# Selective scans on one core: the rows of B and C start 8 bytes further on, and one weight a tile goes to the projections' PSUM bank

## The reference

```
# L1
dts, B, C = split(einsum('bkdl,kcd->bkcl', xs, x_proj_weight))       # 6, 16, 16 rows
delta = softplus(einsum('bkrl,kdr->bkdl', dts, dt_projs_weight) + bias)
h[l] = h[l-1] * exp(delta[l] * A) + (delta[l] * xs[l]) * B[l]         # per d and n
y[l] = sum over n of h[l] * C[l]
# L3
phi = exp(-cumsum(delta * A_log));  dbx = delta * B * xs
h = phi * cumsum(dbx / (phi + 1e-12));  y = einsum('bkdln,bknl->bkdl', h, C)
```

## Time and profile before

| | us |
|---|---|
| three executions | 16074.49, 16085.93, 16095.41; median 16085.93 |
| the profiled execution | 16072.64 |
| its span, from the first to the last instruction | 16070.6 |
| scans of L1, two pairs | 2333 to 5827 and 6058 to 9552 |
| scans of L3, two pairs | 10421 to 12850 and 13363 to 15780 |

### The profile page before, as it was taken

How to read it: one execution, slowest core, us unless ns; L and a number is a source line. 1 busy time by engine, 2 the same in 40 slices (tenths; PEclk the granted TensorE clock), 3 DMA queues, 4 the chain that set the end, 5 groups by cost and what they waited for, 6 DMA issues and landing times. The chain is left out here.

```text
span 16070.6 us, 187344 instructions
## 1 busy us (share of the span) xinstructions
PE 13492.7 (84%) x38048; PEld 5643.9 (35%) x38048; DVE 14447.3 (90%) x19631; ACT 12255.5 (76%) x27077; POOL 11724.6 (73%) x6313
## 2 busy tenths in 40 slices
PE   7998979999999978999999987877777777777777
PEld 2222224444444433444444434433333333333333
DVE  6666649999999989999999985799999989999998
ACT  3555568888888857888888864599999958989996
POOL 0000039999999979999999982388888857888886
PEclk9999989999999989999999997989889888888988
DMA  1100014444444434444444432123333212333221
GB/s 24 21 14 17 5 52 122 121 122 121 120 119 121 120 97 117 121 122 121 121 119 121 120 109 63 54 85 86 85 86 84 86 42 84 87 85 86 84 85 46
DMA packets 543192, 1404.82 MB, mean 87 GB/s; under 512 B 135566, under 2 KB 191926, under 8 KB 539430
## 3 DMA queue, kind: packets, MB, share of 16 engines
q1 hardware_dynamic: 542034, 1392.84, 30.9%
HBM read 1311.24 MB, written 58.30 MB: 85 GB/s over the span
## 5 line engine op out<-in xcount | busy, mean ns | idle before, releaser
L1085 PE MATMUL PS<-Hc,ident 128*128 128x448 f32 x16128 | 7145.1, 579 | 1391.7 <-POOL Hc L1434 1308.2
L1425 POOL TENSOR_TENSOR Tr<-du,BC 128x1344 f32<-128x1344 f32 x2688 | 6894.1, 2565 | 38.0 <-DVE du L1293 36.9
L1085 PEld LDWEIGHTS PS<-Hc,ident 128*128 128x128 f32 x16128 | 3044.4, 199 | 5375.3 <-issue 2719.2
L1434 POOL TENSOR_TENSOR Hc<-Hr,BC 128x896 f32<-128x896 f32 (+1 forms) x2688 | 4049.6, 1507 | 755.0 <-DVE Hr L1343 730.2
L1206 ACT ACTIVATE PS<-dl,A 128x448 f32<-128x448 f32 x5376 | 3399.0, 632 | 976.7 <-DVE Hr L1343 691.2
L1343 DVE TENSOR_TENSOR_SCAN Hr<-PS,Tr 128x449 f32<-128x449 f32 x2688 | 2879.7, 1071 | 1.6 <-ACT PS L1206 0.6
L1343 DVE TENSOR_TENSOR_SCAN PS<-PS,Tr 128x449 f32<-128x449 f32 x2688 | 2830.2, 1074 | 56.3 <-ACT PS L1206 48.5
L1350 DVE TENSOR_TENSOR Hc<-PS,BC 128x448 f32<-128x448 f32 x3584 | 2080.6, 600 | 0.0
L1216 ACT ACTIVATE PS<-cs,lneps,A 128x448 f32<-128x448 f32 x2688 | 1935.7, 720 | 78.3 <-DVE PS L1343 59.0
L1343 DVE TENSOR_TENSOR_SCAN Hr<-Ar,PS 128x449 f32<-128x449 f32 x1792 | 1930.5, 1077 | 0.0
L1325 DVE SCALAR_TENSOR_TENSOR PS<-PS,Tr 128x448 f32<-128x448 f32 x2688 | 1649.3, 614 | 132.6 <-ACT PS L1216 124.4
(11 more groups left out here) (271 smaller groups left out, 15421.6 us busy)
## 6 DMA issues: line engine op xcount, KB each, us to landing
BC<-bcscratch SPq DMA_DIRECT2D x5376, 224.0 KB, 3.6
zscratch<-zst SPq DMA_DIRECT2D x84, 224.0 KB, 1.9
bcscratch<-rows SPq DMA_DIRECT2D x336, 56.0 KB, 1.7
z<-zscratch SPq DMA_DIRECT2D x28, 672.0 KB, 4.9
xg<-mid SPq DMA_DIRECT2D x12, 1176.0 KB, 8.1
xr<-mid SPq DMA_DIRECT2D x56, 168.0 KB, 2.7
rl<-rows SPq DMA_DIRECT2D x56, 168.0 KB, 3.4
Q<-part SPq DMA_DIRECT2D x72, 98.0 KB, 4.3
```

Source lines behind the costliest of these rows:

```text
L1085: e.matmul(PS[:, YB + c, 0:T], K["ident"][:], Hc[:, g % NHC, c, :], start=False, stop=(nn == 15)).then_inc(y_done, 1)
L1425: e.tensor_tensor(Tr[:, g % NTR] if ratio else Tr[:, g % NTR, :, 1:TW], du[:, q % 2], b, ALU.mult).then_inc(t_done, 1)
L1434: e.tensor_tensor(Hc[:, g % NHC, m:3], Hr[:, g % NH, m - 1:2, 1:TW], c_, ALU.mult).then_inc(hp_done, 1)
```

## The change

Three parts, in `scans`:

1. `BC` gets rows of 452 elements, of which elements 2 to 449 are used: each row of B and of C begins 8 bytes behind a multiple of 16. A B row and its C row no longer adjoin in SBUF.
2. What PE writes to the bank XB begins at column 1 instead of 0 (`X`, the projection's rows, and their readers), in both layers.
3. In L3, the weight with s = 30 goes to the bank XB (`SPARE`), and the others share the ring of three. At s = 29 and s = 30 ACT is one unit further ahead with weights and decays, so that two of each are made before the Ln instead of one; `weight_before` gives the weight whose bank a weight takes. `total` of column 0 waits until the scan with s = 30 is done, since it writes over that weight. One memset more zeroes the column 0 of XB.

```diff
-        return PS[:, (XB, HB, 2 if ratio else HB + 1)[c] if q == 0 else XB, 0:T]
+        return PS[:, (XB, HB, 2 if ratio else HB + 1)[c] if q == 0 else XB, 1:1 + T]
...
-        BC = sb("BC", [128, NBS, 2, T])
+        BC = sb("BC", [128, NBS, 2, TP])[:, :, :, 2:2 + T]
...
+        def weight_bank(u):
+            q, r = divmod(u, 48)
+            return XB if r == SPARE else (u - q - (r > SPARE)) % NW
+
+        def weight_before(u):
+            n, back = 0, u
+            while n < NW:
+                back -= 1
+                n += back % 48 != SPARE
+            return back
...
             def total(q, c):
...
+                if ratio and q and c == 0:
+                    e.wait_ge(s_done, 48 * (q - 1) + SPARE + 1)
...
             def weight(u):
...
-                if u >= NW:
-                    e.wait_ge(s_done, u - NW + 1)
+                if u % 48 == SPARE:
+                    e.wait_ge(x_free, use(q + 1, "delta", 2) + 1 if q + 1 < NQS else use(q, "total", 2) + 1)
+                elif u >= NW:
+                    e.wait_ge(s_done, weight_before(u) + 1)
...
-                if ratio and u + 2 < NU:
-                    weight(u + 2)
-                while made < min(u + 3, NU):
+                ahead = u + 4 if ratio and s in (BURST, BURST + 1) and q + 1 < NQS else u + 3
+                while ratio and weighed < min(ahead, NU):
+                    weight(weighed)
+                    weighed += 1
+                while made < min(ahead, NU):
                     decay(made)
                     made += 1
```

More of the change, by code:

```diff
@@ L955, in scans @@
     TW, TP = T + 1, T + 4
+    BURST = 29
+    SPARE = BURST + 1
     NQS = NK * NT
@@ L1015, in input_at @@
         def input_at(g, c):
-            return PS[:, (3 * g + c) % NW, 0:TW] if ratio else Tr[:, g % NTR, c, :]
+            return PS[:, weight_bank(3 * g + c), 0:TW] if ratio else Tr[:, g % NTR, c, :]
         def state_at(g, c, first):
@@ L1035, in proj @@
                 for c in range(3):
-                    a = e.matmul(PS[0:76, XB, 0:T], xp[:, k % 2, c, :], xs[:, c, :], start=(c == 0), stop=(c == 2))
+                    a = e.matmul(PS[0:76, XB, 1:TW], xp[:, k % 2, c, :], xs[:, c, :], start=(c == 0), stop=(c == 2))
                 a.then_inc(x_full, 1)
@@ L1125, in keep_rows @@
                     e.wait_ge(rows_out, 32 * q)
-                e.activation(rows[:], PS[0:64, XB, 0:T], ACT.Copy).then_inc(x_free, 1)
+                e.activation(rows[:], PS[0:64, XB, 1:TW], ACT.Copy).then_inc(x_free, 1)
             def keep_dts(q):
@@ L1131, in keep_dts @@
                 e.wait_ge(x_full, use(q, "proj") + 1)
-                e.activation(dts[:], PS[64:76, XB, 0:T], ACT.Copy)
+                e.activation(dts[:], PS[64:76, XB, 1:TW], ACT.Copy)
             def absolute(q, c):
@@ L1211, in weight @@
                 e.wait_ge(cs_ready, 3 * (q + 1))
-                if u >= NW:
-                    e.wait_ge(s_done, u - NW + 1)
+                if u % 48 == SPARE:
+                    e.wait_ge(x_free, use(q + 1, "delta", 2) + 1 if q + 1 < NQS else use(q, "total", 2) + 1)
+                elif u >= NW:
+                    e.wait_ge(s_done, weight_before(u) + 1)
                 if u == 0:
-                    e.wait_ge(zeroed, 1)
-                e.activation(PS[:, u % NW, 1:TW], cs[:, q % 2, c, :], ACT.Tanh, scale=A2[:, q // NT, c, nn:nn + 1],
+                    e.wait_ge(zeroed, 2)
+                e.activation(PS[:, weight_bank(u), 1:TW], cs[:, q % 2, c, :], ACT.Tanh, scale=A2[:, q // NT, c, nn:nn + 1],
                              bias=K["lneps"][:]).then_inc(w_done, 1)
@@ L1260, in act @@
             e.wait_ge(set_up, 3 if ratio else 1)
-            made = 0
+            made = weighed = 0
             seed(0)
@@ L1323, in input2 @@
                 e.wait_ge(t_done, g + 1)
-                p = PS[:, u % NW, 1:TW]
+                p = PS[:, weight_bank(u), 1:TW]
                 e.scalar_tensor_tensor(out=p, in0=p, scalar=1.0, in1=Tr[:, g % NTR, c, :], op0=ALU.add,
@@ L1368, in dve @@
                 e.memset(PS[:, 0:NW, 0:1], 0.0).then_inc(zeroed, 1)
-            e.wait_ge(zeroed, 1)
+                e.memset(PS[:, XB, 0:1], 0.0).then_inc(zeroed, 1)
+            e.wait_ge(zeroed, 2 if ratio else 1)
             if not ratio:
```

## The result

The changed kernel takes 17274.6 us (median of 4 runs, 17252.1 to 17291.2) against 16082.1 us for the kernel before (4 runs): 1.074 times, 95% interval 1.0721 to 1.0758. The predicted 17264 is 11 us under it. The profiled execution took 17291.2 us, its span is 17289.0.

A forecast was written before the change was run, and what follows sets the result against it. L1's scans were taken as bound by POOL and DVE, both full. Slower products +1218 and part 3 -40 gave +1178 on 16072.6, 17251, as a median 17264 us; own range 17130 to 17350, with other-sign cases 16020 to 17350.

The forecast's parts named there:

- The stage's balance: L1 scans: DVE and POOL both full, so a gain on either gives at most 35 us, a loss counts in full.
- The step of unknown sign: POOL's products with B and C: both operands 8 bytes on run like aligned ones, 0.337 ns an element slower, +1218 us in L1.
- the steady state: POOL's operand streams: after two elements a pair at 8 and 8 stands exactly where one at 0 and 0 does.
- the copies: Single-stream copies at L2593, alternately at a multiple of 16 and 8 behind: neighbours take 0.28 us each, so offset gives no gain.
- Rivals 1 and 2: POOL's products: first, one offset operand is enough, median 16046, chance 0.20; second, both offsets help, 15976 to 16046, chance 0.05.
- rival 4: POOL's products with B and C: a cost per instruction, not per element, +500 us, median 16586, chance 0.07.
- Rival 3: POOL neutral and part 3 gives nothing, the wait at the Ln only moves: about 16086 us, chance 0.08.
- The floor of the Trainium skill: POOL's two-input products: about 2.5 cycles an element as floor by the page, so nothing faster from a second offset.
- the bound: L3 scans: slow products priced at nothing, at most +60 us for both pairs if POOL's lag from du groups reaches DVE.
- what would show it: Signs to check: product durations, L1 stages near 4100 us, L3 near 2409, DVE 85% busy, 1.3 us wait at the Ln.

The follow-up runs named there:

- e4: Changed kernel with delta, du and the states moved back to multiples of 16 bytes, B and C still 8 behind: 16022.5 us against 16077.9 before, ratio 0.9970.
- m1: Separate kernel timing single instructions, eight repeats each, operands at various starts: POOL's 448-element product took 975 to 981 or 1122 to 1128 ns.
- e1: Changed kernel with rows of B and C back at multiples of 16 bytes: 16022.6 us against 16077.9 before, ratio 0.9964; run again in another batch, 16006.9 us.
- g1: Changed kernel with the offset of B and C in L3 alone, in L1 at multiples of 16: 16060.2 us against 16069.2 before, ratio 0.9992.
- e2: Kernel before with only the rows of B and C 8 bytes on: 17306.4 us against 16077.9, ratio 1.0767.
- g2: Changed kernel with B and C 4 bytes behind a multiple of 16 instead of 8: 17260.4 us against 16069.2 before, ratio 1.0741.
- e3: Kernel before with rows of B and C of 452 elements that still begin at multiples of 16 bytes: 16074.6 us against 16077.9, ratio 0.9998.

## Why the prediction was right

**The stage's balance.** It said that a loss on POOL counts in full in L1 and none of it can be absorbed there. POOL was idle for 32 us of that stage before and for 2 now. Without the idle time a pair of groups takes, averaged over the stage, (3493 - 32) / 448 = 7.73 us before and 9.14 now: 1.41 us more (the pairs in the two timelines give 1.43). 448 x 1.41 = 632, less the idle time that took up some 30 us of it, is the stage's 601. The forecast took 1.36 us a pair and let the idle time stand: 609 us. Two errors of a few per cent against each other, the first from long products that came 19 and 12 ns slower than forecast.

**The step of unknown sign.** That two operands 8 bytes on behave as two at multiples of 16 was argued from the steady state of the two streams and from the copies, against the reading that each offset helps. e4 and m1 settle it: what counts is how the two stand to each other. The argument on the steady state was right for this pair; the picture behind it, two streams that must not reach a new 16 bytes at the same time, is not shown, and it would not tell (8, 4) from (4, 8).

**Rivals 1 and 2** fell with the result, and with m1's (8, 8) at 1128 ns, rival 4 with its 1344 elements. Rival 3, part 3 giving nothing, fell with e1.

**The floor of the Trainium skill**, about 2.5 cycles an element for two inputs (GPSIMD Engine Reference, section 2.1; the prediction named section 3.1, which has the 4497 ns), is the slow level here: (3012 - 1127) / 896 = 2.10 ns an element, 2.5 cycles at the page's 1.2 GHz. The fast level, (2563 - 976) / 896 = 1.77 ns, lies under it, so it is no floor.

**What was wrong.** "I price this at nothing, covered by POOL's idle time" for L3: g1 shows 53 us, near the +60 that was the bound. Part of its cause is the one that the bound named, POOL's lag from the groups in which it makes du. But the lag doesn't reach DVE through POOL's own product (DVE's waits for `Tr` are 5.9 us in g1, 5.0 in e1); it does so through PE's order, with the projection behind a sum that waits for POOL. Part 3 was put at -40 and is -55 and -62 us in two batches.

The total is right to 11 us in part by luck. By the lengths of the stages L1 came at +1205 us where the sum had +1218, and L3 at -6 where it had -40: a gain of part 3 larger by some 16 us, and slow products that take some 50 of it back and stood at nothing. Together that is 1199, the medians differ by 1193, and the sum was 1178. So terms that were off by up to 53 us leave 15 in the sum, and 11 in the median, since that of the kernel before came 4 us lower with its fourth run.

**What the sentences on what would show it said.** L1 stages near 4100 us, POOL full, DVE at some 85% and `du<-dl,xs` at 978 ns came as written. The products at 3.0, 2.07 and 1.13 us did so in e2; the changed kernel's own records are longer, for which see the last section. L3's stages near 2409 us did not come: that number was worked from a window that was cut too early, and the gain of 20 us a pair was given back. L3's stages are neither longer than before nor 20 us shorter, so that the sign written down for part 1 alone, "L3's stages longer than before", would not have told of the loss there.

## What to carry to other kernels

- Before a layout is changed for a price seen on one operand, time the pair: one kernel of single instructions with the operands at all starts costs one run, and here it would have told the sign. Then place the operands of POOL's fp32 products so that they start 8 bytes apart, modulo 16, and don't shift both by the same amount.
- An engine with idle time can still be on the path, if an in-order queue stands behind its result and its lag lasts until then. Look at what is queued behind each wait, and for how long the engine stays late after its busiest groups, not at the share of busy time.
- Where two engines are full in one stage, a gain on one is worth at most the other's idle time, and a loss is worth all but the idle time of the engine that loses.

## What the runs showed of the hardware that was not expected

- POOL's two-operand product has two speeds, 976 and 1128 ns for 448 elements and 2563 and 3012 for 1344, by a rule that fits all starts tried, the distance of the operands' starts modulo 16 bytes; and the order counts: 4 and 8 is fast (975 ns, m1), 8 and 4 slow (1125 ns, g2).
- In the changed kernel POOL's recorded durations grow during an L1 stage, from 3.05 us for the input product at its start to 4.04 at its end, while the next product goes on starting 3.0 us after it; its mean of 3347 ns is no cost. In e2, with the same products and L1 stages as long, the mean is 3037, and in g2 3041. Distances from start to start were the safe measure. Why the one grows and the other does not stays open.
- Rows of 1792 bytes instead of 3584, twice the packets, left the landing at 3.7 us against 3.6 and the time the same (e3).
